# A graph network's two softmax stages: chunks laid out by edges instead of by blocks

## The reference

```python
# attention
z = feature @ W_out + b_out
e = gelu((z @ attn_w[:d])[src] + (z @ attn_w[d:])[dst])
ex = exp(e - segment_max(e, dst)[dst])
a = ex / maximum(segment_sum(ex, dst)[dst], 1e-20)
h = segment_sum(a[:, None] * z[src], dst) + (feature @ res_W + res_b)
...
# relation
proj = einsum('ni,rio->nro', nfeat, relation_weight)       # 10 relations
att = sum(proj[src, etype] * tanh(proj[dst, etype] + efeat), axis=-1)
a = exp(att - segment_max(att, dst)[dst]); a = a / segment_sum(a, dst)[dst]
h_nb = segment_sum(nfeat[src] * a[:, None], dst)
out = leaky_relu((nfeat + h_nb) @ res_fc_w.T) + leaky_relu(nfeat * h_nb @ res_fc2_w.T)
```

## Time and profile before

| | us |
|---|---|
| median of 3 runs (4975.91 to 4990.4) | 4976.88 |
| the profiled execution | 4985.03 |
| its span in the trace | 4983.3 |
| attention stage, 1993 to 2619 | 626 |
| relation stage, 2619 to 3960 | 1341 |

### The profile page before, as it was taken

The page is one execution under the profiler, slowest core; times in us unless marked ns, Lnnn a source line. Parts: engine busy times, 40 slices in busy tenths (PEclk is TensorE's granted clock), DMA queues, the critical chain, the costliest instruction groups (busy, mean ns, idle before and its releaser), DMA issues. The chain is left out here.

```text
span 4983.3 us, 76545 instructions
## 1 busy us (share of the span) xinstructions
PE 4090.0 (82%) x23169; PEld 2727.2 (55%) x23381; DVE 3347.1 (67%) x6950; ACT 1944.3 (39%) x3629; POOL 2832.4 (57%) x2859
## 2 busy tenths in 40 slices
PE   5899998999989998477666898988988587777765
PEld 1288887788867777144353444544444444444443
DVE  9967776677668887578776788888887533333332
ACT  0066665444444444023331354554545322222222
POOL 0076664766656665777705444444441167777777
PEclk9999999999989999667758998888988688998899
DMA  1099997999966766355434343433432222222221
GB/s 39 1 282 287 289 286 229 224 229 235 233 173 189 191 188 163 79 128 127 115 74 103 90 102 90 95 94 93 100 90 62 63 62 57 65 65 55 66 65 29
DMA packets 1124509, 648.90 MB, mean 130 GB/s; under 512 B 907542, under 2 KB 940589, under 8 KB 1124104
## 3 DMA queue, kind: packets, MB, share of 16 engines
q1 hardware_dynamic: 1036296, 555.84, 40.8%
q0 software_dynamic: 87808, 88.16, 8.9%
HBM read 384.69 MB, written 261.63 MB: 130 GB/s over the span
## 5 line engine op out<-in xcount | busy, mean ns | idle before, releaser
L2224 POOL DMA_INDIRECT r_got<-x_table,slot_idx x392 | 432.0, 1102 | 717.9 <-DVE r_both_t L2448 308.6
L1092 POOL DMA_INDIRECT o_rows<-in_x_dram,dst_idx x392 | 370.5, 945 | 443.1 <-POOLq L349 241.5
L2539 POOL DMA_INDIRECT m_rows<-x_table,slot_idx x392 | 376.1, 959 | 235.7 <-issue 118.8
L2678 DVE TENSOR_TENSOR_SCAN m_both<-m_keep,m_both,m_rows_t 128x512 f32<-128x512 bf16 x97 | 124.1, 1280 | 561.4 <-PE m_rows_t L2601 561.4
L2323 PE MATMUL r_source_t<-r_masked,rel_pair 64*128 64x512 f32 x980 | 500.3, 659 | 0.0
L2325 PE MATMUL r_own_t<-r_masked,rel_pair 64*128 64x512 f32 x980 | 500.2, 659 | 0.0
L1543 POOL DMA_INDIRECT b_rows<-h_table,slot_idx x392 | 369.7, 943 | 207.1 <-issue 91.5
L1354 POOL DMA_INDIRECT a_got<-node_table,src_idx x392 | 375.4, 958 | 193.6 <-DVE a_conv L1490 55.1
L2003 POOL DMA_INDIRECT t_got<-x_table,slot_idx x392 | 386.2, 985 | 147.3 <-issue 106.7
L2547 POOL DMA_INDIRECT out_dram<-s_res,put_out x392 | 390.6, 996 | 137.0 <-issue 111.1
L2323 PEld LDWEIGHTS r_source_t<-r_masked,rel_pair 64*128 64x128 f32 x980 | 196.2, 209 | 238.8 <-issue 216.8
(11 more groups left out here) (404 smaller groups left out, 11548.0 us busy)
## 6 DMA issues: line engine op xcount, KB each, us to landing
x_table<-n_res SPq DMA_DIRECT2D x196, 256.0 KB
n_rows<-x_table SPq DMA_DIRECT2D x196, 256.0 KB, 3.3
x_table<-s_res SPq DMA_DIRECT2D x294, 128.0 KB
node_table<-n_wide SPq DMA_DIRECT2D x98, 272.0 KB, 4.0
h_table<-n_conv SPq DMA_DIRECT2D x98, 256.0 KB, 3.9
x_table<-s_res SPq DMA_DIRECT2D x98, 256.0 KB
r_feats<-in_edge_attr_dram SPq DMA_DIRECT2D x390, 64.0 KB
n_rows<-in_x_dram SPq DMA_DIRECT2D x97, 256.0 KB, 3.8
```

The lines of the kernel that those rows point to most:

```text
L1092: nc.gpsimd.indirect_dma_start(out=rows[:, n % 4, t, :], out_offset=None, in_=x, in_offset=bass.IndirectOffsetOnAxis(ap=dst_idx[:, n * TIL ...
L2224: nc.gpsimd.indirect_dma_start(out=got[:, n % RING, t, :], out_offset=None, in_=x2_table, in_offset=bass.IndirectOffsetOnAxis(ap=slot_idx[ ...
L2539: nc.gpsimd.indirect_dma_start(out=rows[:, n % 4, t, 0:D], out_offset=None, in_=x3_table, in_offset=bass.IndirectOffsetOnAxis(ap=slot_idx[ ...
```

## The change

Both stages now use chunks of 7 blocks, and a chunk's tiles have a row for each tile of 128 slots: 28 rows by 128 columns in place of 14 or 7 rows by 512. `Softmax.rows` is 28, and the lowest values and carries come for each tile.

The scores of a block are four products: the stationary operand is a 128 by 128 tile of the scan (attention) or of the pair (relation), the moving one a single column. They fill four columns of a PSUM tile of 128 by 28. In attention DVE adds the source's part (`add_scores`), and there are two such PSUM tiles. ACT's `keep` works on 128 by 28 (gelu in attention, copy in relation). PE then turns the scores to 28 by 128 with one transpose (`turn_scores`), into columns 384 to 511 of `f_small_t`, and the shares back with one transpose instead of four. Both stages copy the shares to SBUF (`keep_shares`), attention as the first step of a turn. The turned scores must not overwrite what the chunk ahead still needs, so `turn_scores` waits for that chunk's `shares_kept`.

`X` falls from 25 to 17 in attention, and `RING` and `SCANS` from 29 to 21; in relation it stays 15. The lags of attention's chunk steps change as the lists show. In relation the lists stay, but for `turn_scores`.

```diff
-CHUNK = 14
+CHUNK = 7
...
-            self.score_t = pb(c, "f_score_t", [chunk, EDGE_BLOCK])
+            V_STEPS = 22
+            self.rows = rows = chunk * TILES
+            assert rows <= 64
+            self.score_t = [pb(c, f"f_score_t{h}", [P, rows]) for h in range(score_banks)]
...
+            self.score = self.small_t[0:rows, 384:384 + P]
+            self.kept_score = sb(c, "f_kept_score", [P, 2, rows])
...
-        def keep(self, act, c, func, bias):
-            act.wait_ge(self.scored[c], self.scored.done(c))
+        def keep(self, act, c, func, scores, made, bias=None):
+            act.wait_ge(made[c], made.done(c))
+            if c >= 2:
+                act.wait_ge(self.scores_turned[c - 2], self.scores_turned.done(c - 2))
+            if bias is not None:
+                nc.scalar.activation(self.kept_score[:, c % 2, :], scores, func, bias=bias).then_inc(self.kept[c], 1)
+            else:
+                nc.scalar.activation(self.kept_score[:, c % 2, :], scores, func).then_inc(self.kept[c], 1)
+
+        def turn_scores(self, pe, c):
+            pe.wait_ge(self.kept[c], self.kept.done(c))
             if c >= 1:
-                act.wait_ge(self.belows[c - 1], self.belows.done(c - 1))
-            if bias is not None:
-                nc.scalar.activation(self.score[:, :], self.score_t[:, :], func, bias=bias).then_inc(self.kept[c], 1)
-            else:
-                nc.scalar.activation(self.score[:, :], self.score_t[:, :], func).then_inc(self.kept[c], 1)
+                pe.wait_ge(self.shares_kept[c - 1], self.shares_kept.done(c - 1))
+            nc.tensor.transpose(self.score, self.kept_score[:, c % 2, :], ident[:, :]).then_inc(self.scores_turned[c], 1)
...
-            for t in range(TILES):
-                to = self.share_t[c % 2][:, t, :] if self.share_t else self.small_t[:, 128 + t * self.chunk:128 + (t + 1) * self.chunk]
-                last = nc.tensor.transpose(to, self.share[:, t * P:(t + 1) * P], ident[0:self.chunk, 0:self.chunk])
-            last.then_inc(self.shares_turned[c], 1)
+            nc.tensor.transpose(self.small_t[:, 320:320 + self.rows], self.share[:, :], ident[0:self.rows, 0:self.rows]).then_inc(self.shares_turned[c], 1)
...
-        X = CHUNK + 11
+        X = CHUNK + 10
...
-            soft = Softmax(c, CHUNK, False, True)
+            soft = Softmax(c, CHUNK, False, 2)
...
-                    over_turns((load, 0, BLOCKS), (load_soft, 0, BLOCKS), soft.after(11, soft.store_betas, sp), (load_betas, X, BLOCKS),
+                    over_turns((load, 0, BLOCKS), (load_soft, 4, BLOCKS), soft.after(10, soft.store_betas, sp), (load_betas, X, BLOCKS),
...
-                        if n % CHUNK == 0:
-                            if n // CHUNK - 1 >= 0:
-                                pe.wait_ge(soft.kept[n // CHUNK - 1], soft.kept.done(n // CHUNK - 1))
-                        nc.tensor.matmul(soft.score_t[:, :], soft.slide(score_cols, n), scan[:, n % SCANS, :],
-                                         start=(n % CHUNK == 0), stop=False, skip_group_check=True)
+                        if n // CHUNK >= 2:
+                            pe.wait_ge(score_added[n // CHUNK - 2], score_added.done(n // CHUNK - 2))
+                        for t in range(TILES):
+                            last = nc.tensor.matmul(soft.score_at(n, t), scan[:, n % SCANS, t * P:(t + 1) * P], score_col[:, :],
+                                                    start=True, stop=True, skip_group_check=True)
                         if n % CHUNK == CHUNK - 1:
-                            k = n // CHUNK
-                            pe.wait_ge(score_kept[n], score_kept.done(n))
-                            for t in range(TILES):
-                                last = nc.tensor.matmul(soft.score_t[:, t * P:(t + 1) * P], source_score[:, k % 2, t, :], ident[:, :],
-                                                        start=False, stop=True, skip_group_check=True)
-                            last.then_inc(soft.scored[k], 1)
+                            last.then_inc(soft.scored[n // CHUNK], 1)
...
-                               soft.after(4, soft.turn_ends, pe), soft.after(5, soft.turn_peaks, pe),
+                               soft.after(4, soft.turn_scores, pe), soft.after(5, soft.turn_ends, pe), soft.after(6, soft.turn_peaks, pe),
                                soft.after(8, soft.turn_sums, pe), soft.after(9, soft.turn_totals, pe),
-                               soft.after(11, turn_shares, pe))
+                               soft.after(10, turn_shares, pe))
...
+                    def keep_shares(eng, k):
+                        soft.keep_shares(eng, k, weighed, (k - 1) * CHUNK - 1)
+
+                    def add_scores(eng, k):
+                        dve.wait_ge(soft.scored[k], soft.scored.done(k))
+                        dve.wait_ge(score_kept[k * CHUNK + CHUNK - 1], score_kept.done(k * CHUNK + CHUNK - 1))
+                        if k >= 2:
+                            dve.wait_ge(soft.kept[k - 2], soft.kept.done(k - 2))
+                        nc.vector.tensor_tensor(whole_score[:, k % 2, :], soft.scores_of(k),
+                                                source_score[:, k % 2].rearrange("p j t -> p (j t)"), ALU.add).then_inc(score_added[k], 1)
...
-                    over_turns((invert, X + 3, BLOCKS), (weigh, X, BLOCKS), (sum_up, 1, BLOCKS + X), (match_source, 1, BLOCKS), (mask, X + 3, BLOCKS),
+                    over_turns(soft.after(10, keep_shares, dve), (invert, X + 3, BLOCKS), (weigh, X, BLOCKS), (sum_up, 1, BLOCKS + X), (match_source, 1, BLOCKS), (mask, X + 3, BLOCKS),
                                (scale, X + 3, BLOCKS), (powers, X + 2, BLOCKS), (keep_score, 1, BLOCKS),
-                               soft.after(4, soft.raise_rows, dve), soft.after(5, soft.run_peaks, dve),
+                               soft.after(2, add_scores, dve), soft.after(4, soft.raise_rows, dve), soft.after(5, soft.run_peaks, dve),
                                soft.after(6, soft.enter_peaks, dve), soft.after(6, soft.raise_all, dve), soft.after(6, soft.soften, dve),
-                               soft.after(8, soft.sum_rows, dve), soft.after(9, soft.copy_fades, dve),
-                               soft.after(9, soft.run_totals, dve), soft.after(10, soft.enter_totals, dve),
-                               soft.after(10, soft.sum_all, dve), soft.after(10, soft.share_out, dve))
+                               soft.after(7, soft.sum_rows, dve), soft.after(8, soft.copy_fades, dve),
+                               soft.after(8, soft.run_totals, dve), soft.after(9, soft.enter_totals, dve),
+                               soft.after(9, soft.sum_all, dve), soft.after(9, soft.share_out, dve))
...
-            soft = Softmax(c, CH, True, False)
+            soft = Softmax(c, CH, True, 1)
...
-                        if n % CH == 0:
-                            if n // CH - 1 >= 0:
-                                pe.wait_ge(soft.kept[n // CH - 1], soft.kept.done(n // CH - 1))
-                        last = nc.tensor.matmul(soft.score_t[:, :], soft.slide(ones_cols, n), pair[:, n % 2, :],
-                                                start=(n % CH == 0), stop=(n % CH == CH - 1), skip_group_check=True)
+                        if n >= CH and n % CH == 0:
+                            pe.wait_ge(soft.kept[n // CH - 1], soft.kept.done(n // CH - 1))
+                        for t in range(TILES):
+                            last = nc.tensor.matmul(soft.score_at(n, t), pair[:, n % 2, t * P:(t + 1) * P], ones[:, 0:1],
+                                                    start=True, stop=True, skip_group_check=True)
...
-                               (add_up, X + 4, BLOCKS), soft.after(6, soft.turn_peaks, pe), soft.after(8, soft.turn_totals, pe),
+                               (add_up, X + 4, BLOCKS), soft.after(5, soft.turn_scores, pe), soft.after(6, soft.turn_peaks, pe), soft.after(8, soft.turn_totals, pe),
```

More of the change, by code:

```diff
@@ L177, in build @@
     lows_f = [dram(f"lows_f{k}", (SLOTS,)) for k in range(2)]
-    row_low = [dram(f"row_low{k}", (BLOCKS,)) for k in range(2)]
+    row_low = [dram(f"row_low{k}", (COLS,)) for k in range(2)]
     root9 = dram("root9", (9, SLOTS), BF16)
@@ L1692, in __init__ @@
             self.small_t = pb(c, "f_small_t", [P, 512])
-            self.share_t = [pb(c, f"f_share_t{h}", [P, TILES, chunk]) for h in range(2)] if many_shares else None
-            self.score = sb(c, "f_score", [chunk, EDGE_BLOCK])
-            self.low = sb(c, "f_low", [chunk, 2, EDGE_BLOCK])
-            self.same = sb(c, "f_same", [chunk, 2, EDGE_BLOCK])
-            self.peak = sb(c, "f_peak", [chunk, EDGE_BLOCK + 1])
-            self.below = sb(c, "f_below", [chunk, EDGE_BLOCK])
-            self.fall = sb(c, "f_fall", [chunk, EDGE_BLOCK])
@@ L1708, in __init__ @@
[L1708 to L1710 removed]
+            self.score = self.small_t[0:rows, 384:384 + P]
```

(22 more changed lines are left out.)

123 lines of the change are left out of this document (56 added, 67 removed).

## The result

The changed kernel takes 4847.59 us (median of 3 runs, 4830.43 to 4851.29) where the kernel before takes 4976.88: a ratio of 0.9738, interval 0.9715 to 0.976, some 130 us less. The profiled execution took 4830.43, at the lower end of its runs, where that of before had been above its median.

What follows compares the result with a forecast made beforehand. POOL's gathers set attention's pace; in relation PE bound plain turns, DVE softmax turns. Gains of 141 (relation) and 43 (attention) summed to 184: 4801 profiled, 4793 median, said as 4790; eight in ten between 4712 and 4890.

Steps and rivals of the forecast that it cites:

- Attention: Attention stage: gains 43 us, between 25 and 55, from a shorter tail and gathers, with POOL still bounding the middle.
- The gathers: POOL's gathers in attention: 0 to 10 us of their stretched time may come back, taken as 5.
- the tail's term: DVE's turns after attention's last gather: 17 × 3.46 = 58.8 plus 10 for one softmax, 69 us instead of 107.
- Relation: Relation stage: gains 141 us as taken, up to 210 with no fall of PE's clock.
- the operation L1847: DVE operation in relation's softmax: 1.96 us instead of 0.68, unexplained; its extra 1.28 was allowed to stay in part.
- 3 us for the softmax: Each relation chunk: the narrower softmax keeps 3 of its 19 us, provided PE keeps its clock.
- 4 for the clock: Each relation chunk: PE's clock falls about once, in the shares' turn, costing 4 us.
- The two ends: Relation's two end chunks: they keep half of their 24 us, 12; 15 were taken off for early turns.
- A fall: A drop of PE's clock in a relation turn, when PE idles without the wide score product: costs 4.1 to 4.8 us.
- The 15 us given for the early turns: Relation's eleven early turns with the score product before: clock falls in some, 15 us lost in all (0 to 45).
- The rival in which the clock falls in every turn: Relation: PE's clock falls in each turn, +105 us, about 5080, slower; chance 0.07.
- the end of 0.87: Relation's score product on PE: four one-column products take at most 0.87 us, costing nothing in a plain turn.

Runs made afterwards that it cites:

- attn_x23: The changed kernel with attention's X at 23 instead of 17; POOL's wait after the last gather is 107.07 us instead of 87.23.
- slid28_pair_early: The changed kernel with both a 28-row score product streaming 512 columns in relation and POOL's product moved between a block's first two gathers; 4744.91 us, ratio 0.9538.
- pool_short: The changed kernel with POOL's product in relation cut to 8 of its 512 columns, the rest left out; 4789.79 us in one run.
- pair_early: The changed kernel with POOL's product in relation moved between a block's first and second gather; 4787.47 us, ratio 0.9626.
- slid28: The changed kernel with relation's scores coming 28 by 128 straight from PE, 28-column stationary window, 512 columns streamed, no score transpose; 4806.09 us, ratio 0.965.

## Why the prediction was right or wrong

The forecast was 4790, its range 4712 to 4890; 4847.59 lies inside, the gain of 129 at 69% of the 187 forecast. The direction and the places were right, and one term was not.

**Attention: right, and nearly term by term.** 43 us forecast. From the first gather to the last scan it took 617.4 before and 574.1 after, 43.2 less. The last 17 turns take 69.8, where 17 × 3.46 and 10 for the softmax gave 69. The gathers gave 11.5 instead of 5, and 5.4 go back since DVE is later behind the last gather than it was (8.3 us from its end to the scan, where it was 2.9). POOL bounds the middle as it did. attn_x23 shows the tail's term by itself.

**Relation: 108 in this trace instead of 141, and the step that failed is the operation L1847.** The working gave a chunk 3 us for the softmax and 4 for the clock, 7 of 19, and had 9.2 to explain. By the runs: the softmax itself costs 2.8 (slid28_pair_early: 72.56 against 69.7), as forecast; POOL's product costs 3.8 (pool_short: 78.9 to 75.1), of which the held operations themselves are some 2.9 (the four groups shown for pair_early), where the working, in its own words "I do not know why", let some of its 1.28 stay and took 0.3 for the whole turn; the rest, 2.6, is the clock once the holds are gone: the one turn of 13.79 us in place of 11.30.

The parts do not stand quite by themselves, since a held turn is late and a late turn lets PE idle. In the trace after, the 83 turns from the 15th to the 98th scan are 76 us longer than in slid28_pair_early: 20 in 60 turns at the full clock, 56 in 23 turns below it, which hold falls and held operations together. So the clock cost between 2.6 and 4.7 a chunk, and the 4 taken for it are not refuted.

The error was to scale an excess with the length of the operation that showed it. It belonged to what ran beside it, had the length of that, 1.28, and passed to whichever operation came next once L1847 was short. Over the 83 turns 107 us are left above plain ones where 84 were counted, 23 of the 33 missing. Another 12 are that 12 × 19 = 228 was counted where this stretch, 1042.3 us before, held 216 above 83 plain turns. The two ends, level instead of 3 worse, give 3 back.

**The clock.** A fall was priced at 4.1 to 4.8. By the turns it is less: 1.66 in an early turn, 1.6 and 3.3 in the two turns of pair_early, 2.5 in pool_short; there are more of them, 21 in the 81 turns of the body behind the first two. What goes with it, from the trace after: PE's join behind 1.35 us of idle time, and a product at the lower level and one back at the upper, with the one-column products of an earlier turn in the first row:

```profile
2906.31 1.05 PE L2346 MATMUL f_score_t<-ones,r_pair 128*128 128x1 f32 x8 [0.18 <-POOL r_pair L2245]
...
2939.20 0.78 PE L2320 MATMUL r_both_t<-ident,r_got 128*64 128x128 f32 x4 [1.35 <-ACT r_scan L2390]
...
2945.09 1.06 PE L2335 MATMUL r_source_t<-r_masked,rel_pair 64*128 64x512 f32 x1
...
2946.56 0.59 PE L2335 MATMUL r_source_t<-r_masked,rel_pair 64*128 64x512 f32 x1
```

Here the lower level follows a wait of 1.35, where the row of before showed one of 4.55. The 15 us given for the early turns came out by luck: some of eleven were to fall, at 4.1 each, and all nine without softmax work fell, at 1.6, some 14 in all. With the first chunk's softmax, shorter by 5, and the tail, which gained 8.6, the ends came out level instead of 3 us worse. That the form of the score product does it, and not other work, slid28 shows in the early turns; in the chunks it changed nothing until POOL's product had been moved. The rival in which the clock falls in every turn did not come: plain turns stayed at 9.96. The rule on bursts that was weighed for it, from the Trainium skill (TensorE: Matmul & The Clock Gate, section HAM oscillation), is borne out here by the early turns (0.83 each) and a part of the softmax turns (0.67 to 0.86) alone.

**The one-column products** take 0.95 to 1.05 us for four, above the end of 0.87 that was set from products of 64 columns; eight instructions of 0.13 each. The upper end of that bound was no bound. It cost little: the join still waits for ACT's copy in most turns, and in 9 it waits for these products instead, 2.8 us in all between 2720 and 3640.

**The level of the runs.** 8 us were taken off to go from the profiled run to the median; the profiled run after was 17 below its own median. That is 25 of the 55 between 4793 and 4848, and no step of the sum; the other 30 are the 184 forecast for the two stages against the 154.6 of the traces.

## What to carry to other kernels

When one operation takes longer than its like, look at what the other engines do at that instant before scaling it: an excess that ends when a neighbour ends has the neighbour's length, and will move to another operation when you shorten this one. Placing the neighbour against work that doesn't conflict gave 50 us in one kernel and 55 in the other for two moved lines. And a product that is hidden is not free to shrink: here PE kept its clock through a wait of 1.3 to 1.4 us with the one form and lost it with the other, and a form that moves as many columns for the same result (28 columns of weights, 128 moved) was worth 36 us over the cheaper-looking one.

## What was not expected of the hardware

A product of POOL from SBUF (128 by 512, 1.27 us) holds a DVE operation of 128 by 4 for up to 1.6 us; the DVE operations here with one of their operands in PSUM (maskings of 128 by 512, scans of the turns) run beside it without loss. Four fp32 products with a 128 by 128 stationary operand and one moving column take 0.95 to 1.05 us at the upper clock, as long as four with 28 stationary columns and 128 moving ones (1.06). And PE's busy time does not tell its clock: 483 busy us of 583 in attention after at 0.50, against 401 of 626 before at 0.68.
